# A fused attention and quantized FFN kernel on one core: the prologue and the first three pipeline steps replanned

## What is computed

```python
def reference(x, idx1, bias_table, idx2, w1, Wq, Wk, Wv, Wo, w2, w_up, w_down):
    h = einsum('bct,bcd->bdt', x, w1[idx1]) + bias_table[idx1][:, :, None]
    q, k, v = (split_heads(h @ W.T) for W in (Wq, Wk, Wv))
    scores = einsum('bhqd,bhkd->bhqk', q, k) / sqrt(32) + alibi
    x = x + merge_heads(softmax(scores) @ v) @ Wo.T
    g = einsum('bct,bcd->bdt', x, w2[idx2])
    for w in (w_up, w_down):                 # hbitlinear(g, w)
        s = max(mean(abs(w)), EPS)           # one number per weight
        wq = clip(round(w / s), -1, 1) * s
        gq = act_quant(fwht(g), 8)
        g = gq @ wq.T                        # after w_up: square(relu(.))
    return x + g
```

## Time and profile before

| | |
|---|---|
| median of 3 executions | 771.02 us (769.98 to 771.21) |
| profiled execution | 770.51 us |
| its span, first to last instruction | 768.7 us |
| PE busy | 724.3 us, 94% of the span |
| DVE, ACT, POOL busy | 663.8, 425.7, 218.7 us |
| mean granted TensorE clock | 0.978 of full speed |

### The profile page before, as it was taken

The page is one execution under the profiler, slowest core; times in us unless marked ns, Lnnn a source line. Parts: engine busy times, 40 slices in busy tenths (PEclk is TensorE's granted clock), DMA queues, the critical chain, the costliest instruction groups (busy, mean ns, idle before and its releaser), DMA issues.

```text
span 768.7 us, 23147 instructions
## 1 busy us (share of the span) xinstructions
PE 724.3 (94%) x9627; PEld 614.7 (80%) x9660; DVE 663.8 (86%) x1339; ACT 425.7 (55%) x847; POOL 218.7 (28%) x231
## 2 busy tenths in 40 slices
PE   6878699999999999999999999999999999998767
PEld 3867588888888888888888888888888888886543
DVE  3644899999999999999999999999999999899876
ACT  2656565655665565665565556565566556555421
POOL 1222123333332223333333222333333222223300
PEclk8989799999999999999999999999999999999999
DMA  8641011111101111111111111111110110010000
GB/s 281 223 134 36 1 36 50 50 49 50 49 23 44 36 50 49 50 49 50 49 33 36 47 37 50 49 50 50 50 48 23 59 31 24 23 29 18 15 14 27
DMA packets 37388, 39.90 MB, mean 52 GB/s; under 512 B 21156, under 2 KB 21284, under 8 KB 37284
## 3 DMA queue, kind: packets, MB, share of 16 engines
q1 hardware_dynamic: 34436, 33.48, 14.1%
q10 hardware_dynamic: 2848, 4.95, 1.8%
HBM read 30.02 MB, written 8.39 MB: 50 GB/s over the span
## 4 chain that ended last, share of the span: by engine, by line
PE 85%; DVE 5%; POOL 3%; issue 3%; ACT 2%; DMA 1%; SPq 1%; POOLq 0%; DVEq 0%
PE bank L354 44%; PE bank L478 8%; PE bank L514 7%; PE bank L460 4%; PE bank L378 4%; PE bank L344 4%; PE bank L487 4%; PE bank L418 3%; PE bank L435 3%; POOL gT L260 3%; PE bank L468 1%; PE bank L498 1%; DMA bias_in<-in_fside_8xS_dram 1%; DVE hid L260 1%; DVE hid L929 1%
## 5 line engine op out<-in xcount | busy, mean ns | idle before, releaser
L260 POOL TENSOR_TENSOR gT<-gT 128x256 f32<-128x256 f32 x124 | 107.9, 890 | 446.0 <-ACT gT L650 443.5
L260 DVE TENSOR_TENSOR hid<-hid 128x512 f32<-128x512 f32 x128 | 100.6, 827 | 0.0
L625 ACT ACTIVATE v_kd<-bank 64x256 f32<-64x256 f32 x128 | 48.5, 379 | 71.3 <-PE bank L354 70.2
L354 PE MATMUL bank<-h_hi,wk_hi 128*128 128x256 f32 x256 | 76.0, 297 | 3.2 <-POOL h_lo L1058 3.2
L354 PE MATMUL bank<-h_hi,wq_hi 128*128 128x256 f32 x256 | 74.3, 290 | 0.0
L478 PE MATMUL bank<-q1T,up_w 128*128 128x128 bf16 x1024 | 65.4, 224 | 9.2 <-DVE q1T L876 9.2
L354 PE MATMUL bank<-h_lo,wk_hi 128*128 128x256 f32 x256 | 73.1, 286 | 0.0
L354 PE MATMUL bank<-h_hi,wk_lo 128*128 128x256 f32 x256 | 73.0, 285 | 0.0
L661 ACT ACTIVATE late<-bank 128x512 f32<-128x512 f32 x64 | 37.6, 588 | 62.5 <-PE bank L478 62.5
L478 PEld LDWEIGHTS bank<-q1T,up_w 128*128 128x128 bf16 x1024 | 59.7, 100 | 14.8 <-DVE q1T L876 9.8
L354 PE MATMUL bank<-h_hi,wq_lo 128*128 128x256 f32 x256 | 71.5, 279 | 0.0
(11 more groups left out here) (117 smaller groups left out, 1933.1 us busy)
## 6 DMA issues: line engine op xcount, KB each, us to landing
x_in<-in_x_dram SPq DMA_DIRECT2D x32, 256.0 KB, 2.7
x_res<-in_x_dram SPq DMA_DIRECT2D x32, 256.0 KB, 3.3
out_dram<-late SPq DMA_DIRECT2D x32, 256.0 KB, 3.4
w_in<-in_L_cond_weights_dram SPq DMA_DIRECT2D x126, 16.0 KB, 2.3
bias_in<-in_fside_8xS_dram SPq DMA_DIRECT2D x62, 32.0 KB, 2.9
k_bd<-in_L_attn_Wk_dram ACTq DMA_DIRECT2D x1, 1024.0 KB, 5.6
s<-in_L_attn_Wq_dram ACTq DMA_DIRECT2D x1, 1024.0 KB, 8.5
v_kd<-in_L_attn_Wv_dram ACTq DMA_DIRECT2D x1, 1024.0 KB, 10.7
```

The source lines that it names most:

```text
L260: eng.tensor_tensor(dv[:, :, n], sv[:, :, 0], sv[:, :, 1], op).then_inc(done, 1)
L354: mm = pe.matmul(dst, lhs(a, k), rhs(b, k), start=(k == 0 and n == 0), stop=(k == KC - 1 and n == 2))
L625: ins = act.activation(v_kd[b * T:b * T + T, c % 4, e], blocks[e * T:e * T + T, :, b, :], ACT.Copy)
```

## The change

Nothing of the result changes. What each engine does before and in steps 0 to 2 is put in another order and in part on other engines:

- Loads: the constants (`cst_sb` and the position bias) move from ACT's queue, behind the weights, to SP's, once the inputs of pairs 0 and 1 are there. `wq` and `wv` wait for the same inputs instead of for `wk`. The up weight moves from SP to ACT. `wo` goes last, in three pieces to other buffers (`x1`, `gT`, `gT2`). Indices are read ahead of the wait.
- ACT does one tiny activation early. `h_lo` of pair 1 goes to DVE. The first job is written out in another order (all products with `h_lo` last), with 7 throwaway matmuls ahead of it.
- The absolute sums of the up weight go from ACT to DVE, ahead of step 0. The sum over partitions goes from POOL (`w_reduce`) to PE (`w_total`, a matmul with one column of ones), for both weights.
- `w_round(0, .)` moves ahead of step 0; `wo` is split at the end of step 0; `clip_high(0)` moves into step 1, `clip_low(1, 1)` and `clip_high(1)` into step 2.
- On PE, `v_product(0)` goes right behind `scores(0)`, and `qk(1, 0)` ahead of `o_product(0)`.

```diff
@@ scalar (ACT), prologue
-            act.wait_ge(s_wraw["wk"], 16)
-            for name, src in (("wq", wqT), ("wv", wvT), ("wo", woT)):
-                load_w(name, src)
-            act.dma_start(cst_sb[:, H * T:], cst[:, H * T:]).then_inc(s_cst, 16)
-            act.dma_start(flat(pT), cst[:, 0:H * T]).then_inc(s_cst, 16)
+            act.wait_ge(s_cin1[0], 80)
+            act.wait_ge(s_cin1[1], 80)
+            load_w("wq", wqT)
+            load_w("wv", wvT)
             copy_hi(0)
             copy_hi(1)
+            load_ffn_weight(act, 0, 0)
             split_w("wq")
-            for job in range(4):
+            copy_qk(1, 0, 0, bank[2])
+            load_ffn_weight(act, 0, 1)
+            load_w("wo", woT)
+            split_w("wv")
+            for job in range(1, 4):
                 copy_qk(job + 1, 0, job, bank[2 + job % 2])
...
-            w_abs_sum(0, 0)
-            w_abs_sum(0, 1)
+            copy_hi(3)
+            w_round(0, 0)
+            w_round(0, 1)
@@ tensor (PE)
+            def w_total(n):
+                pe.wait_ge(s_cst, 16)
+                pe.wait_ge(s_fsum, 3 * n + 1)
+                pe.matmul(ps_total, wsum[:, n, 5:6].broadcast_to([P, P]), had[:, 0:1], start=True, stop=True).then_inc(s_ftotal, 1)
...
                 if pair(c):
                     scores(c)
+                if c == 0:
+                    w_total(0)
+                    v_product(0)
@@ vector (DVE), prologue, then the ends of steps 0, 1 and 2
             lo_part("wq", a_whi, 1)
-            hi_part("wo")
-            lo_part("wo", d_whi, 2)
             lo_part("wv", a_whi, 2)
...
+                w_abs_sum(0, c - 2)
...
                 if c == 0:
                     clip_low(0, 0)
                     clip_low(0, 1)
+                    hi_part("wo")
+                    lo_part("wo", d_whi, 4)
+                if c == 1:
                     clip_high(0)
-                if c == 1:
-                    w_scale(1)
                     clip_low(1, 0)
-                    clip_low(1, 1)
+                if c == 2:
                     clip_high(1)
@@ gpsimd (POOL)
-            def w_reduce(n):
-                pool.wait_ge(s_fsum, 3 * n + 1)
-                pool.partition_all_reduce(wsum[:, n, 2:3], wsum[:, n, 5:6], P, RADD).then_inc(s_ftotal, 1)
-                pool.wait_ge(s_ftotal, n + 1)
```

More of the change, by code:

```diff
@@ L522, in first_cond1, with next_cond1, first_job @@
                 cond1(c)
+            def next_cond1(c):
+                pe.wait_ge(s_cin1[c % 2], (c // 2 + 3) * 80)
+                pe.wait_ge(d_h, c + AHEAD)
+                pe.wait_ge(d_alibi, 2 * c + 2)
+                cond1(c + AHEAD)
+            def first_job():
+                for n, (w, h) in enumerate(((w_hi, h_hi), (w_lo, h_hi), (w_hi, h_lo))):
+                    if n == 2:
+                        pe.wait_ge(p_hlo, 2)
+                        pe.wait_ge(d_hlo1, 1)
+                    for k in range(KC):
+                        mm = pe.matmul(bank[2][:, 0:GT], w["wk"][:, k, 0:P], h[:, 0, k, :], start=(n == 0 and k == 0),
+                                       stop=(n == 2 and k == KC - 1))
+                mm.then_inc(s_qk, 1)
             first_cond1(0)
             first_cond1(1)
-            pe.wait_ge(p_hlo, 2)
-            for job in range(8):
+            keep_clock(7, y1[:, :].bitcast(BF16), bank[3])
+            pe.wait_ge(s_wlo, 1)
+            pe.wait_ge(a_hhi, 2)
+            first_job()
+            for job in range(1, 8):
                 if job % KC == 0:
@@ L554, in _ @@
                     hadamard2(c - 2, 1)
-                if next_group(c):
+                if next_group(c) and c != 1:
                     qk(c, 0)
[L557 to L560, removed]
-                    cond1(c + AHEAD)
+                if pair(c + AHEAD) and c > 0:
+                    next_cond1(c)
                 if pair(c - 1):
                     cond2(c - 1)
-                if pair(c):
+                if pair(c) and c > 0:
                     v_product(c)
+                if c == 0:
+                    next_cond1(c)
                 if next_group(c):
                     qk(c, 1)
+                if c == 1:
+                    w_total(1)
                 if c == NPAIR:
@@ L977, in _ @@
                     less_max(c, 1)
-                if c == 0:
-                    w_total(0)
+                if c == 2:
+                    clip_low(1, 1)
                 if pair(c - 2):
@@ L1003, in _ @@
                     fly2(c - 2)
-                if pair(c + AHEAD):
+                if pair(c + AHEAD) and c > 0:
                     dve.wait_ge(p_hlo, c + 3)
```

168 lines of the change are left out of this document (93 added, 75 removed).

## The result

The changed kernel takes 763.21 us (median of 4 executions, 762.34 to 764.45), the kernel before, beside it on the same chip, 770.5 us (768.47 to 771.21). The ratio is 0.9913, 95% interval 0.9891 to 0.9935. So it is faster, and inside the range, but by about 7 us where 15 were forecast. The profiled execution has a span of 761.9 us and took 763.7 us.

A forecast was written before the change was run, and what follows sets the result against it. PE, busy 94% of the span, bounds the kernel, so what counts is how early it reaches the steady rhythm. `up(0)` 14.6 to 16.6 us earlier, plus step 2, gives 15.0: 770.5 - 15.0 = 755.5 us, range 749 to 764.

The forecast's parts named there:

- three signs of being wrong: `scores(0)` later than before; steps 1 and 2 over 22 us; or a longer steady step.
- Inputs and first job: Prologue: last bias lands at 9.0 us, first job begins at 12.0 against 17.53, a gain of 5.5 us there.
- The copy queue: Prologue: job 2 waits for ACT's copy behind `wq`'s split, about 3 us idle; `scores(0)` at 31 to 33 us.
- The gain of 0.5 to 2.5 us for the prologue: Prologue alone: `scores(0)` starts at 31 to 33 us against 33.44 before.
- Step 0: `turn_p(0, 0)` 9.5 us after `scores(0)` instead of 16.0, without POOL's standing still; `scores(1)` at 45.3 to 47.3.
- Step 1: `scores(1)` to `scores(2)`: `wo` split and ACT's added work cost 1.7 us, 20.0 instead of 18.3.
- `up(0)`: Last long-waiting PE group of the prologue: starts at 66.6 to 68.6 us, 14.6 to 16.6 ahead of 83.21.
- Step 2: `up(0)` to `up(1)`: full clock gains, added DVE clips cost; 0 together, range -0.6 to +1.0 us.
- steps of 21.44 from then on: From step 3 onward: lists unchanged, so each steady step still takes 21.44 us.
- My rival of a longer steady step: Steady steps: PE waits once per step as POOL's and DVE's work coincide; 0.8 us per step, 779 us; 3%.
- the copy queue and the clock eat more: Rival, prologue and steps 0 and 1: late `wq`, `wv` and low clock cost 3 to 8 us; 762 us; 17%.

The follow-up runs named there:

- a_copies: Changed kernel with ACT's copies of jobs 0 to 3 put ahead of the weight splits and loads: 757.59 us, ratio 0.9826 to the kernel before.
- a_hold: Changed kernel with SP's position bias and inputs of pairs 2 and 3 held back until `wv` has landed: 760.56 us, ratio 0.9861 to the kernel before.
- a_pool: Changed kernel with the two sums over partitions put back on POOL: 778.92 us, ratio 1.0105 to the kernel before.
- b_pesum: Kernel before with only the sums over partitions moved from POOL to PE (`w_total`): 767.86 us, ratio 0.9937 to the kernel before.
- a_wo: Changed kernel with `wo` split by DVE in the prologue instead of at the end of step 0: 766.57 us, ratio 0.9920 to the kernel before.
- b_pad: Kernel before with only the unused 4-byte tile `first_act` declared early: 773.62 us, ratio 1.0035 to the kernel before.
- a_last: Changed kernel with the tile `first_act` declared behind all other tiles: 759.00 us, ratio 0.9828 to the kernel before.
- a_tail: Changed kernel with throwaway matmuls in PE's idle places of steps 30, 31 and 32: 760.22 us, ratio 0.9857 to the kernel before.

## Why the prediction was wrong

The mechanisms before step 2 were right, except that `wv` had no landing of its own. The sum of them was 3 us too high, and the last steps and the steady step, where it said that nothing changes, took 5 us. Two of its own three signs of being wrong came: `scores(0)` later than before, and a longer steady step. In the order of its steps:

- *Inputs and first job, 12.0 us:* measured 12.82. Right but for 0.9 us: the last bias took 4.02 us to land and not 3.1, so `wq` and `wv` were issued 0.9 us later too. In the twelve variants with the same lists up to there the first job began at 12.15 to 13.65, once at 14.65.
- *The copy queue, job 2 at 17.3 to 18.8, job 3 at about 22.5, `scores(0)` at 31 to 33:* measured 18.89, 24.60 and 34.83. The queue was right (a_copies), but **this term was mis-sized**: I priced `wq`'s landing by single loads of 1 MB (6.7 us, within my 6 to 7.5) and gave `wv` none of its own, as if it were there when ACT reached it. It lands 11.94 us after its issue, 3.9 us of it because the position bias and the inputs of pairs 2 and 3 share the engines (a_hold); the page of before had 10.7 us for it. On top, PE's idle times of 2.54 and 2.79 us were followed by the lower level of the clock. Against the middle of my range `scores(0)` came 2.8 us late: 0.9 by the start, 1.2 by `wv`, and about 0.7 because from job 3 to `scores(0)` PE took 10.2 us instead of 8.3 and the 1.1 that I took for the clock. No run holds the clock alone. The gain of 0.5 to 2.5 us for the prologue was a loss of 1.4.
- *Step 0:* 14.06 us from `scores(0)` to `scores(1)`, forecast 14.3. The absolute sum 2.28 us (2.29), idle 0.64 (0.8), `w_total` 0.35 us (0.3), `turn_p` 9.4 us after `scores(0)` (9.5). Right. POOL's standing still was the price (a_pool), but b_pesum shows that it can't be had alone.
- *Step 1, 20.0 us:* measured 21.17. The `wo` split is 2.2 us (a_wo) where I took 1.1 to 1.3 for it; that the two lower clips ahead of it took 4.2 us beside POOL and not 2 x 1.22 would account for the rest, but no run takes POOL's work away there.
- *`up(0)`:* waited for nothing and ran at full clock, as said, but at 71.24 and not at 66.6 to 68.6: 3.6 us behind the middle of that range. The sum had taken 0.6 us off the gain there, which leaves the 3.1.
- *Step 2:* 21.99 us, before 21.88; forecast 0 between. Right: `up(0)` at full clock gave back 1.6 us (1.96 against 3.59), and PE waited for DVE instead (1.20 us for `sq_lo`).
- *"steps of 21.44 from then on":* **this step failed.** The lists are unchanged, but each step took 0.07 us more, 1.7 us over 24 steps, by where the new tile is declared (b_pad, a_last). The diff had the line, and I gave it no price. My rival of a longer steady step had the right place, another mechanism, and needed 0.52 us per step.
- *The last steps:* **no step of the prediction looks at them,** which took them as unchanged. They took 3.1 us more than before, at the lower level of the clock after idle times that are in both kernels (a_tail). The median of the eleven unfilled kernels is 83.4 us, so both ends of the comparison, 81.8 and 84.9, are partly chance.

Together: 15.0 - 3.1 (at `up(1)`) - 0.2 (the steps behind `up(1)` and `up(26)`) - 1.7 (steady) - 3.1 (last steps) - 0.1 (behind `up(31)`) = 6.8 us, the difference of the spans. The rival "the copy queue and the clock eat more" gave 762 us. It had the right time by luck, more than half of it for another reason: the prologue and step 1 cost 3.1 us, what lay behind `up(2)` 5.

The Trainium skill (GPSIMD Engine Reference, Engine selection: partition reductions belong on GpSimd) speaks against the sum on PE, and the runs here disagree with it: 0.40 us of work brings 6.28 and 6.96 us of standing still with it, the matmul 0.35 us; a_pool's span is 15.1 us longer than the changed kernel's.

What stays open: by what rule a tile's place in memory costs time on PE, and why the lower level of the clock follows the same idle times in one execution and not in another.

## What to carry to other kernels

When work is moved forward in a prologue, walk each load's landing separately and with everything issued in the same stretch, not by a median; then look what stands behind its consumer in that engine's list. A gain at the start is only at the end if nothing in between changes: compare the mean duration of the same instruction group in the steady step of both kernels, and try a new small tile behind all others. A mark of one profiled execution moves with its inputs' landing: compare from a common start. Idle times of 2 to 3 us in the last steps are worth filling with throwaway matmuls where nothing else can be put there.

## What the hardware showed that I hadn't expected

- A tile of four more bytes declared ahead of the operand tiles lengthens the 128x256 matmuls `bank<-h_lo,wk_hi` from 279 to 282 ns and the 128x512 ones `bank<-wo_lo,oT_hi` from 389 to 394 ns, 0.06 to 0.07 us per step; 64 bytes do the same (281 and 395 ns, 0.09 us).
- A DVE lower clip of 128x2048 (f32 to bf16) took 1.22 us alone, 1.93 and 2.30 us while POOL ran two-operand work.
- Of two loads of 1 MB issued 0.47 us apart, the second landed 11.94 us after its issue with 1.2 MB of SP's loads beside it (position bias 512 KB, two inputs of 256, four biases of 32, four weights of 16), 7.9 us with these held back. The first half of the up weight moved beside it too; without that it took 11.8 us.
- Behind three idle times of 2.56 to 3.16 us at the end the lower level of the clock follows in some executions and not in others: the same four steps took 81.8 to 88.0 us in eleven kernels, 81.5 to 81.6 us in the five where these places are filled.
